# One pass over eight batches instead of two passes over four

## The chip, the cores and the metric

The kernel runs on one core of a Trainium2 chip. The time is the device time of one execution in microseconds (us), and the median of several runs is quoted. Five engines run their own streams of instructions and meet through semaphores: TensorE (PE, with its weight loads PEld), VectorE (DVE), ScalarE (ACT), GpSimd (POOL) and SyncE (SP), which issues the transfers here.

## The reference

x has 8 batches of 512 rows of 128 channels. Three layers are added onto it, each on the layer-normalised x:

```python
x = x + 0.5 * ffn(layernorm(x))       # FFN 1
x = x + latent_attention(layernorm(x))  # MLA
x = x + 0.5 * ffn(layernorm(x))       # FFN 2, same weights as FFN 1
```

Each ffn has two layers. One layer shifts half of the channels by one row, projects to q, k, v (8 heads of 64), normalises q and k, rotates them, attends in windows of 64 rows (this one and the one before), projects back and adds, then normalises and runs a gated feed-forward part of 341 hidden channels. The latent attention has 16 heads of 8 channels, a latent of 64, and full causal attention over the 512 rows. Nothing is exchanged between batches.

## The kernel before

**Staging.** Weights are loaded and prepared once, in a setup block. Then comes a hardware loop, line 1223, with B // NB = 2 rounds. X, the running activations, and U, the normalised copy and the ffn's own running value, hold NB = 4 batches in SBUF, NS = NB * NT = 16 slots of 128 rows. One round loads four batches (line 328), runs `ffn_phase`, `mla_phase` and `ffn_phase` on them, and stores them (line 335). Each phase is a block of its own with a barrier between all engines behind it, and `clear_all` (line 109) ends the round with semaphore clears and one more barrier. The loop body is written once in the program and run twice.

**The ffn phase.** A unit is one slot in one of the two layers; there are NU = 2 * NS = 32 units in a phase, all slots of layer 0 and then all of layer 1. `STEPS = range(NU + 7)`: a software pipeline written out by hand. In step n every engine does a piece of unit n, of n-1, and so on down to n-7, in an order fixed in the code. So the first steps fill the pipeline and the last seven drain it. On DVE a unit passes, among others, RA and RB (rotation, lines 647 and 651), SS (sum of squares over q and k, line 719, in step u+2), KT (740), the row maxima NMX (630), ON (756), GLU (685), and the new value of its slot, U (727, step u+7); in layer 1 the update of X follows (731). POOL does the sums RA, the powers RN and RV and the scalings. Two edits depend on the slot count: `norm_stats` of slot u+NT runs in steps with u+NT < NS, and `norm_apply` in steps NT <= u < NS, both on DVE. A slot of layer 1 waits for the U of the same slot in layer 0, which is NS units back.

**The MLA phase.** Per batch there are GROUPS = 4 groups of four heads, and per group UN = 11 score tiles. The phase runs ALLU = NB * 4 * 11 tiles and YT_LAG + 1 = 12 steps more. In the first group of a batch DVE also makes the norm of the next batch; XT, values, queries and keys of the next one are prepared between tiles. Before the first tile the first batch's norm, transpose, values, queries and keys run one after the other.

Ring buffers (RA, PT, KT and V for two batches, PSUM banks) do not depend on NB.

Of the kernel before, what the change touches and what calls it, by code (L numbers as in the profile page):

```python
# [16 lines left out]
P = 128  # L17
# [5 lines left out]
LG = 4  # L23
# [26 lines left out]
def macaron(nc, x, W_dq, W_uq, W_dkv, W_uk, W_uv, W_o, wqkv, q_scale, k_scale, wo, ln_g, ln_b,  # L50
            w1, b1, w2, b2, consts, out):
    B, T, C = x.shape
    DEPTH, HID = w2.shape[0], w2.shape[1]
    NT = T // P
    NB = 4
    NS = NB * NT
    QL = W_dq.shape[0]
    HC = -(-HID // 3)
# [4 lines left out]
    with top:  # L63
# [3 lines left out]
        def sb(name, shape, dt=F32):  # L67
            return stack[-1].enter_context(nc.sbuf_tensor(f"{name}_{phase[0]}", shape, dt))
# [3 lines left out]
        def sem(name, kind="setup"):  # L72

            if (kind, name) not in sems:
                sems[kind, name] = top.enter_context(nc.semaphore(f"{name}_{kind}"))
            return sems[kind, name]
# [2 lines left out]


        ROPE = NT * 4 * DH
        cst = sb("cst", [P, ROPE + 4 * P + LG + 2])
        ident = cst[:, ROPE + 3 * P:ROPE + 4 * P]
        headsel = cst[:, ROPE + 4 * P:ROPE + 4 * P + LG]
        low_rows = cst[:, ROPE + 4 * P + LG:ROPE + 4 * P + LG + 2]
        maskb = sb("maskb", [P, 3, P], BF16)
        identb = sb("identb", [P, P], BF16)
        ropet = sb("ropet", [P, DEPTH, NT, 4, DH])
# [20 lines left out]
        def clear_all(used):  # L109

            engines = (nc.sync, nc.tensor, nc.scalar, nc.vector, nc.gpsimd)
            for n, s in enumerate(used):
                engines[n % len(engines)].sem_clear(s)
            nc.all_engine_barrier()


        with ExitStack() as scope:
            stack.append(scope)
            qs = sb("qs", [P, DEPTH, 2, DH])
            ks = sb("ks", [P, DEPTH, DH])  # L120
            dq = sb("dq", [QL, P]); uq = sb("uq", [P, QL]); dkv = sb("dkv", [QL, P])
# [9 lines left out]
            with nc.Block() as block:  # L131
                @block.sync
                def _(sp):
                    def load(dst, src):
                        sp.dma_start(dst, src).then_inc(loaded, 16)
                        LOADS[0] += 16
                    load(cst[:, :], consts)
                    load(dq[:, :], W_dq); load(uq[:, :], W_uq); load(dkv[:, :], W_dkv)
                    load(uk[:, :], W_uk); load(uv[:, :], W_uv); load(wom[:, :], W_o)
                    load(wqkv_raw[:, :, :], wqkv.rearrange("l p n -> p l n"))  # L140
                    load(w1_s[:, :, :], w1.rearrange("l p n -> p l n"))
                    for l in range(DEPTH):
                        load(wo_s[:, l, :, :], wo[l].rearrange("(c p) n -> p c n", p=P))
                    for c in range(3):
                        load(w2_s[0:HCS[c], :, c, :], w2[:, c * HC:c * HC + HCS[c], :].rearrange("l p n -> p l n"))
                    load(b1row[:, :], b1.rearrange("l (e h) -> (l e) h", e=2))
                    load(lnrow[0:DEPTH, :], ln_g)
                    load(lnrow[DEPTH:2 * DEPTH, :], ln_b)
                    load(b2_s[:, :, :].rearrange("p l n -> p (l n)"),
                         b2.rearrange("(a l) n -> a (l n)", a=1).broadcast_to([P, DEPTH * P]))  # L150
                    load(qs[:, :, 0, :], q_scale.unsqueeze(0).broadcast_to([P, DEPTH, DH]))
                    load(qs[:, :, 1, :], k_scale.unsqueeze(0).broadcast_to([P, DEPTH, DH]))
# [47 lines left out]
                @block.vector  # L200
                def _(dve):

                    dve.wait_ge(loaded, NL)
                    nc.vector.tensor_copy(maskb[:, :, :], cst[:, ROPE:ROPE + 3 * P].rearrange("p (a b) -> p a b", a=3))
                    nc.vector.tensor_copy(identb[:, :], ident)
                    dve.wait_ge(mm, 3)
                    nc.vector.tensor_copy(lncol[:, :], BK[7][:, 0:2 * DEPTH]).then_inc(columns, 1)
                    for c in range(3):
                        last = nc.vector.tensor_copy(b1raw[0:HCS[c], c, :], BK[7][0:HCS[c], 8 * (c + 1):8 * (c + 1) + 2 * DEPTH])
                    last.then_inc(columns, 1)  # L210

                    def stacked(bank):
                        return bank[:, 0:P].rearrange("p (g e) -> p g e", g=GROUPS).unsqueeze(2) \
                            .to_broadcast([P, GROUPS, 4, LG * DG])

                    for n, (dst, src, factor) in enumerate([
                            (uqT[:, :], BK[0][0:QL, 0:P], 1.0), (woT[:, :], BK[1][:, 0:P], 1.0),
                            (WqT[:, :], BK[3][:, 0:P], 1.0),
                            (Wq_s[:, :, :, :], stacked(BK[4]), float(DG) ** -0.5),
                            (ve[:, :], BK[5][0:QL, 0:P], 1.0), (keT[:, :], BK[6][0:QL, 0:P], 1.0),  # L220
                            (Wv_s[:, :], BK[0][:, 0:P], 1.0), (Wk_s[:, :, :, :], stacked(BK[1]), 1.0)]):
                        dve.wait_ge(mm, [1, 2, 4, 5, 6, 7, 8, 9][n])
                        nc.vector.tensor_scalar(dst, src, factor, None, ALU.mult).then_inc(copied, 1)
                    for l in range(DEPTH):

                        tab = cst[:, 0:ROPE].rearrange("p (t f d) -> p t f d", t=NT, f=4)
                        for f in range(4):
                            sc = qs[:, l, f // 2, :]
                            if f % 2:
                                for hf in range(2):  # L230
                                    other = sc[:, (1 - hf) * 32:(1 - hf) * 32 + 32]
                                    nc.vector.tensor_tensor(
                                        ropet[:, l, :, f, hf * 32:hf * 32 + 32], tab[:, :, f, hf * 32:hf * 32 + 32],
                                        other.unsqueeze(1).to_broadcast([P, NT, 32]), ALU.mult)
                            else:
                                nc.vector.tensor_tensor(ropet[:, l, :, f, :], tab[:, :, f, :],
                                                        sc.unsqueeze(1).to_broadcast([P, NT, DH]), ALU.mult)
                    dve.wait_ge(mm, 10)
                    dve.wait_ge(columns, 2)
                    for l in range(DEPTH):  # L240
                        for c in range(3):
                            j = l * 6 + c
                            nc.vector.tensor_tensor(b1_s[0:HCS[c], l, :, c], BK[2][0:HCS[c], j:j + 4:3],
                                                    b1raw[0:HCS[c], c, 2 * l:2 * l + 2], ALU.add)

                        nc.vector.tensor_scalar(w1_s[:, l, :], w1_s[:, l, :], lncol[:, l:l + 1], None, ALU.mult)
# [24 lines left out]

        def ffn_phase(it, load, store, used):
            with ExitStack() as scope:
                stack.append(scope)

# [28 lines left out]
                    "w1a_in w1g_in gl_ok glu_ok w2_in u3_ok dch st nvar_ok nrstd_ok u_ok x_ok stored").split()}  # L306
                x_in = [sem(f"x_in{b}", "ffn") for b in range(NB)]
                NU = DEPTH * NS
# [14 lines left out]
                with nc.Block() as block:  # L323
                    @block.sync
                    def _(sp):
                        if load:
                            for b in range(NB):
                                sp.dma_start(X[:, b * NT:(b + 1) * NT, :],
                                             x[it * NB + b].rearrange("(t p) c -> p t c", p=P)).then_inc(x_in[b], 16)
                        for last_use in used:  # L330
                            sp.sem_clear(last_use)
                        if store:
                            for b in range(NB):
                                sp.wait_ge(S["x_ok"], NT * (b + 1))
                                sp.dma_start(out[it * NB + b].rearrange("(t p) c -> p t c", p=P),
                                             X[:, b * NT:(b + 1) * NT, :]).then_inc(S["stored"], 16)
                            sp.wait_ge(S["stored"], 16 * NB)

# [881 lines left out]
                phase[0] += 1  # L1220
                return list(S.values())

        with nc.Fori(0, B // NB, 1) as it:
            used = ffn_phase(it, load=True, store=False, used=[])
            used = mla_phase(used)
            clear_all(ffn_phase(it, load=False, store=True, used=used))


# [26 lines left out]
```

## Time and profile before

| | us |
|---|---|
| median of 3 runs | 2463.88 (2462.53 to 2465.33) |
| span of the profiled execution | 2459.3 |
| median less span | 4.6 |

| engine | busy us | share of the span |
|---|---|---|
| DVE | 2183.2 | 89% |
| PE | 2129.6 | 87% |
| ACT | 1663.2 | 68% |
| POOL | 1246.0 | 51% |

The page gives the span of the profiled execution, from the first to the last instruction, and no other time of it; the 4.6 us to the median lie around it. Busy is time in which an engine works on an instruction. The program has six phases that stand apart in the trace: ffn, MLA, ffn, and the same again, so a share of the whole span mixes three kinds of work with their beginnings and ends; the windows by phase are to be read instead.

### The profile page before, as it was taken

The numbers are of one execution on the slowest core, as the hardware profiler recorded it, in microseconds if no ns is written. First come the engines' busy times: TensorE is split into PE (matmuls) and PEld (weight loads), VectorE is DVE, ScalarE is ACT, GpSimd is POOL, SyncE is SP. The second block draws the span as 40 slices with busy tenths as digits, with TensorE's granted clock in tenths as the row PEclk, the third lists the DMA queues.
The fourth block names the chain that finished last, engine by engine and source line by source line (L and its number), as shares of the span: only waits on it lengthen the run. The fifth ranks groups of instructions, "written<-read, shape, count | busy, mean of one in ns | idle before, by whom it ended". The sixth has DMA issues, their size and how long they took to land. (4 is left out here: it accounts for less than half of the span.)

```text
span 2459.3 us, 58228 instructions
## 1 busy us (share of the span) xinstructions
PE 2129.6 (87%) x20074; PEld 1666.7 (68%) x20074; DVE 2183.2 (89%) x5134; ACT 1663.2 (68%) x3674; POOL 1246.0 (51%) x1048
## 2 busy tenths in 40 slices
PE   2888899879997988989968988998799978898997
PEld 2677777756664777777747777777466657777776
DVE  4999999968887999999969999998688879999997
ACT  1676767648895666776726677676588846777675
POOL 3656655523224565655545565564232256565553
PEclk9999999979998999999979999999899989999999
DMA  2000000000000000000000000000000000000000
GB/s 89 1 2 2 2 2 1 2 1 1 2 1 1 1 2 2 1 2 10 6 23 2 2 1 2 2 2 1 1 2 1 1 1 1 2 2 2 6 6 10
DMA packets 12619, 12.41 MB, mean 5 GB/s; under 512 B 1397, under 2 KB 11687, under 8 KB 12327
## 3 DMA queue, kind: packets, MB, share of 16 engines
q1 hardware_dynamic: 12327, 8.63, 1.2%
q8 instruction: 170, 2.79, 0.5%
q14 instruction: 122, 1.00, 0.1%
HBM read 6.53 MB, written 2.10 MB: 4 GB/s over the span
## 5 line engine op out<-in xcount | busy, mean ns | idle before, releaser
L847 POOL TENSOR_TENSOR RN<-SS,mhalf 128x16 f32<-128x16 f32 x128 | 374.9, 2929 | 19.1 <-DVE SS L721 19.0
L838 POOL TENSOR_TENSOR U2B<-U,b_s 128x128 f32<-128x128 f32 x128 | 61.3, 479 | 569.7 <-DVE U L727 555.4
L539 ACT ACTIVATE PR<-bank,NMX 128x128 f32<-128x128 f32 x1024 | 290.1, 372 | 56.3 <-DVE NMX L632 51.9
L596 ACT ACTIVATE GL<-bank,b_s 114x128 f32<-114x128 f32 (+1 forms) x384 | 113.3, 366 | 251.7 <-PE bank L386 251.7
L377 PE MATMUL bank<-KT,QZ 128*64 128x128 f32 x4096 | 280.5, 279 | 0.0
L377 PEld LDWEIGHTS bank<-KT,QZ 128*64 128x64 f32 x4096 | 218.7, 137 | 70.0 <-issue 70.0
L1092 ACT ACTIVATE PL<-bank,NM 128x384 f32<-128x384 f32 (+3 forms) x512 | 255.9, 542 | 14.0 <-DVE NM L1170 11.2
L1170 DVE TENSOR_REDUCE NM<-bank 128x1 f32<-128x384 f32 (+3 forms) x352 | 217.3, 635 | 38.6 <-PE bank L1006 34.9
L386 PE MATMUL bank<-HN,w_s 128*114 128x128 f32 (+1 forms) x1536 | 222.9, 282 | 0.0
L362 PE MATMUL bank<-wqkv_h,HTH 128*128 128x512 f32 x384 | 196.9, 513 | 11.1 <-DVE HTL L707 11.0
L1015 PE MATMUL bank<-cst,PL 128*128 128x128 f32 x1280 | 200.1, 275 | 3.9 <-ACT PTL L1084 1.9
L386 PEld LDWEIGHTS bank<-HN,w_s 128*114 128x114 f32 (+1 forms) x1536 | 186.2, 180 | 19.9 <-issue 19.9
L1001 PE MATMUL bank<-KL,QZL 128*128 128x384 f32 (+3 forms) x512 | 190.5, 425 | 4.6 <-DVE QZL L1129 4.6
L578 ACT ACTIVATE PT<-bank 128x512 f32<-128x512 f32 x128 | 76.5, 597 | 160.8 <-PE bank L444 160.4
L630 DVE TENSOR_REDUCE NMX<-bank 128x4 f32<-128x512 f32 x256 | 174.8, 683 | 10.8 <-PE bank L377 9.5
L647 DVE TENSOR_TENSOR RA<-bank,ropet 128x512 f32<-128x512 f32 x256 | 174.5, 681 | 9.0 <-PE bank L362 4.8
L353 PE MATMUL bank<-cst,RA 128*128 128x128 f32 x1024 | 163.6, 285 | 12.2 <-POOL RA L858 11.3
L651 DVE TENSOR_TENSOR RB<-bank,ropet 128x512 f32<-128x512 f32 x256 | 173.6, 678 | 0.0
L1210 POOL TENSOR_SCALAR QZL<-QS,cst 128x512 fp32r<-128x512 f32 x64 | 108.1, 1699 | 128.7 <-DVE QS L1119 128.5
L1084 ACT ACTIVATE PTL<-bank 128x512 f32<-128x512 f32 (+1 forms) x288 | 162.1, 563 | 13.9 <-PE bank L1015 10.4
L476 PEld LDWEIGHTS bank<-VA,PT 128*64 128x64 f32 x2048 | 135.6, 143 | 48.7 <-issue 48.7
L830 POOL TENSOR_TENSOR RA<-RA,RB 128x512 f32<-128x512 f32 x128 | 162.1, 1267 | 10.8 <-DVE RB L651 10.8
(159 smaller groups left out, 6238.9 us busy)
## 6 DMA issues: line engine op xcount, KB each, us to landing
X<-in_L_attn_x SPq DMA_DIRECT2D x8, 256.0 KB, 4.3
out<-X SPq DMA_DIRECT2D x8, 256.0 KB, 2.3
wqkv_raw<-in_L_ffn_wqkv SPq DMA_DIRECT2D x1, 1536.0 KB
cst<-shape_constants SPq DMA_DIRECT2D x1, 771.0 KB
w_s<-in_L_ffn_w SPq DMA_DIRECT2D x1, 682.0 KB
wo_s<-in_L_ffn_wo SPq DMA_DIRECT2D x2, 256.0 KB
w_s<-in_L_ffn_w SPq DMA_DIRECT2D x2, 114.0 KB
b_s<-in_L_ffn_b SPq DMA_DIRECT2D x1, 128.0 KB
```

What stands on the lines that cost most here:

```text
L362: last = nc.tensor.matmul(BK[B_QKV[k]][:, :], h[:, bb, tok].bitcast(F32R), w[:, l, cols].bitcast(F32R), start=(n == 0), stop=(n == 2))
L377: last = nc.tensor.matmul(BK[B_S[g]][w * W:(w + 1) * W, (h % 4) * P:(h % 4 + 1) * P], QZ[:, h, w * W:(w + 1) * W], KT[:, h // 2, bb, k0:k0 ...
L386: last = nc.tensor.matmul(BK[k][0:HCS[j], j * P:(j + 1) * P], w1_s[:, l, o:o + HCS[j]], HN[:, :], start=True, stop=True)
L539: last = nc.scalar.activation(PR[:, 4 * g + h, :], BK[B_S[g]][:, h * P:(h + 1) * P], ACT.Exp, bias=NMX[:, 4 * g + h:4 * g + h + 1], scale=8.0)
L630: link(nc.vector.tensor_reduce(c, BK[B_S[g]][:, :].rearrange("p (h q) -> p h q", h=4), AX_X, ALU.max))
L647: nc.vector.tensor_tensor(RA[:, u % 2, g, :, :], src, ropet[:, l, t, 2 * g, :].unsqueeze(1).to_broadcast([P, NH, DH]), ALU.mult)
L651: nc.vector.tensor_tensor(RB[:, g, :, :].rearrange("p h (z d) -> p h z d", z=2), rot, tab.unsqueeze(1).to_broadcast([P, NH, 2, DH // 2]), ...
L847: nc.gpsimd.tensor_tensor(RN[:, u % 2, :], SS[:, :], mhalf[:, 0:2 * NH], ALU.pow).then_inc(S["rn_ok"], 1)
L1001: nc.tensor.matmul(bank[:, h * N:(h + 1) * N], QZL[:, G % 2, h0 + h, i * P:(i + 1) * P].bitcast(F32R), KL[:, G % 2, 0:N].bitcast(F32R), st ...
L1015: last = pe.transpose(BK[B_PT[k % 2]][:, j * P:(j + 1) * P], PL[:, k % PRING, j * P:(j + 1) * P], ident)
L1092: last = nc.scalar.activation(PL[:, m % PRING, h * N:(h + 1) * N], BK[m % SRING][:, h * N:(h + 1) * N], ACT.Exp, bias=NM[:, m % SRING, h:h ...
L1170: nc.vector.tensor_reduce(NM[:, m % SRING, 0:n], BK[m % SRING][:, 0:n * N].rearrange("p (h k) -> p h k", h=n), AX_X, ALU.max, negate=True) ...
```

## The change

NB becomes B = 8: the hardware loop and its `it` index are gone, and each phase is written out for 32 slots, 64 ffn units and 352 tiles of latent attention. The loads and stores address x[b] and out[b] directly. X and U are twice as large in SBUF; to make room the rotation table is loaded into a tile `rope` of its own, which lives only during setup, with one more load.

```diff
-    NB = 4
+    NB = B
...
-        cst = sb("cst", [P, ROPE + 4 * P + LG + 2])
-        ident = cst[:, ROPE + 3 * P:ROPE + 4 * P]
+        cst = sb("cst", [P, 4 * P + LG + 2])
+        ident = cst[:, 3 * P:4 * P]
...
+            rope = sb("rope", [P, ROPE])
...
-                    load(cst[:, :], consts)
+                    load(rope[:, :], consts[:, 0:ROPE])
+                    load(cst[:, :], consts[:, ROPE:])
...
-                        tab = cst[:, 0:ROPE].rearrange("p (t f d) -> p t f d", t=NT, f=4)
+                        tab = rope[:, :].rearrange("p (t f d) -> p t f d", t=NT, f=4)
...
-        def ffn_phase(it, load, store, used):
+        def ffn_phase(load, store, used):
...
-                                             x[it * NB + b].rearrange("(t p) c -> p t c", p=P)).then_inc(x_in[b], 16)
+                                             x[b].rearrange("(t p) c -> p t c", p=P)).then_inc(x_in[b], 16)
...
-                                sp.dma_start(out[it * NB + b].rearrange("(t p) c -> p t c", p=P),
+                                sp.dma_start(out[b].rearrange("(t p) c -> p t c", p=P),
...
-        with nc.Fori(0, B // NB, 1) as it:
-            used = ffn_phase(it, load=True, store=False, used=[])
-            used = mla_phase(used)
-            clear_all(ffn_phase(it, load=False, store=True, used=used))
+        used = ffn_phase(load=True, store=False, used=[])
+        used = mla_phase(used)
+        clear_all(ffn_phase(load=False, store=True, used=used))
```

Where it moves instructions is shown at three places. First the end of the last ffn phase on SP, with the waits of each row: before, each round ends with four stores, clears, and the branch back to the loads.

```order
L331 ISA x29
L335 ISA [waits x_ok_ffn]
L335 DMA out<-X 128x4x128
...
L323 UNCONDITIONAL_BRANCH [waits stored_ffn]
L113 ISA [waits barrier_Pool_Activation_PE_DVE_SP_release]
L113 ISA x13
L1223 REGISTER_ALU [waits barrier_Pool_Activation_PE_DVE_SP_release]
L1223 COMPARE_AND_BRANCH
```

The same place now, where the eight stores of the single pass follow each other and nothing branches back:

```order
L333 ISA x29
L337 DMA out<-X 128x4x128 [waits x_ok_ffn] x8
L325 UNCONDITIONAL_BRANCH [waits stored_ffn]
L113 ISA [waits barrier_Pool_Activation_PE_DVE_SP_release]
L113 ISA x14
```

One store wait, one barrier and the branch in the middle of the run are gone. Second, DVE at the last update of X of batch 3 in the second ffn phase (slot 15); X is written at L731 before and at L733 after. Before, the pipeline has drained and DVE has the last units' GLU, U and X alone:

```order
L701 TENSOR_TENSOR HN<-bank,DT 128x128
L727 TENSOR_TENSOR U<-bank,U2B 128x128
L731 SCALAR_TENSOR_TENSOR X<-U,X 128x128
L685 SCALAR_TENSOR_TENSOR GLU<-bank,b_s,GL 114x128 x2
L685 SCALAR_TENSOR_TENSOR GLU<-bank,b_s,GL 113x128
L727 TENSOR_TENSOR U<-bank,U2B 128x128
L731 SCALAR_TENSOR_TENSOR X<-U,X 128x128
L323 UNCONDITIONAL_BRANCH
```

Now the work of later slots stands around the same update:

```order
L709 TENSOR_TENSOR HTL<-bank,HTH 64x128 x2
L662 COPY HT_3<-bank 64x128
L663 COPY HT_3<-bank 64x128
L721 TENSOR_REDUCE SS<-SQ 128x16
L723 TENSOR_SCALAR SS<-SS 128x16
L729 TENSOR_TENSOR U<-bank,U2B 128x128
L733 SCALAR_TENSOR_TENSOR X<-U,X 128x128
L742 COPY KT<-bank 128x4x128
L757 RECIPROCAL RS<-bank 128x4
L758 TENSOR_TENSOR ON<-bank,RS 128x256
```

Seven draining steps, and the filling ones behind them, have become full steps. Third, DVE in the MLA phase at the end of batch 3 (OTL is the copy of a group's result, Y its division, NM a row maximum). Before:

```order
L1170 TENSOR_REDUCE NM<-bank 128x1 x3
L1190 RECIPROCAL RL<-bank 128x16
L1193 TENSOR_TENSOR Y<-bank,RL 128x128
L1179 COPY PTL<-bank 128x4x128 x2
L1185 COPY OTL<-bank 128x512
L1190 RECIPROCAL RL<-bank 128x16
L1193 TENSOR_TENSOR Y<-bank,RL 128x128
L934 UNCONDITIONAL_BRANCH
```

Now:

```order
L1172 TENSOR_REDUCE NM<-bank 128x1
L1187 COPY OTL<-bank 128x512
L271 TENSOR_SCALAR U<-X,mv,rstd 128x128
L1172 TENSOR_REDUCE NM<-bank 128x1
L271 TENSOR_SCALAR U<-X,mv,rstd 128x128
L1172 TENSOR_REDUCE NM<-bank 128x1
L271 TENSOR_SCALAR U<-X,mv,rstd 128x128
L1172 TENSOR_REDUCE NM<-bank 128x1
L1192 RECIPROCAL RL<-bank 128x16
L1195 TENSOR_TENSOR Y<-bank,RL 128x128
```

The copy of batch 3's last result now stands among tiles and norm steps of the batches behind it.

## Rows read from the trace of the kernel before

**Rows 1.** The page: busy time by engine, and the clock in slices.

```profile
PE 2129.6 (87%) x20074; PEld 1666.7 (68%) x20074; DVE 2183.2 (89%) x5134; ACT 1663.2 (68%) x3674; POOL 1246.0 (51%) x1048
PEclk9999999979998999999979999999899989999999
```

**Rows 2.** Windows: us, busy (count) of PE, PEld, DVE, ACT, POOL; granted clock, DMA share, GB/s.

```profile
42.10:517.90 475.80, 413.64 (x4128) 341.08 (x4128) 445.18 (x1088) 313.79 (x699) 275.22 (x233) 0.98 0.01 3
517.90:767.80 249.90, 232.68 (x1760) 147.54 (x1760) 195.37 (x377) 200.68 (x437) 68.02 (x54) 0.95 0.01 1
767.80:1244.60 476.80, 414.85 (x4128) 342.08 (x4128) 445.13 (x1087) 313.70 (x699) 275.84 (x233) 0.96 0.01 3
1244.60:1254.20 9.60, 0.00 (x0) 0.00 (x0) 0.00 (x0) 1.23 (x1) 0.00 (x0) 0.55 0.28 72
1254.20:1730.20 476.00, 414.64 (x4128) 341.11 (x4128) 446.45 (x1088) 313.95 (x700) 275.44 (x233) 0.97 0.01 3
1730.20:1980.00 249.80, 232.60 (x1760) 147.29 (x1760) 194.84 (x376) 200.66 (x437) 68.33 (x54) 0.95 0.01 1
1980.00:2453.90 473.90, 411.81 (x4128) 339.57 (x4128) 444.67 (x1087) 313.89 (x699) 275.92 (x233) 0.97 0.01 3
```

**Rows 3.** Windows: one ffn batch, its drain, one MLA batch, its start.

```profile
96.20:153.90 57.70, 51.76 (x518) 42.40 (x517) 55.39 (x139) 40.72 (x90) 32.75 (x27) 0.98 0.01 2
478.20:517.90 39.70, 34.66 (x346) 29.50 (x344) 27.58 (x86) 20.08 (x45) 10.38 (x12) 0.92 0.01 1
618.20:675.20 57.00, 56.45 (x441) 35.87 (x441) 47.92 (x94) 50.04 (x110) 16.64 (x13) 1.00 0.01 2
518.40:542.30 23.90, 12.68 (x34) 7.26 (x35) 11.20 (x29) 5.70 (x12) 7.24 (x6) 0.50 0.00 1
```

**Rows 4.** Tile SS on DVE, five starts a window: ns min/median/max, first and last start.

```profile
L719 DVE TENSOR_REDUCE SS<-SQ x5: 1219/1219/1220, 96.2 to 153.9; 128x16 f32<-128x1024 f32 x5
L719 DVE TENSOR_REDUCE SS<-SQ x5: 1219/1220/1222, 267.1 to 322.3; 128x16 f32<-128x1024 f32 x5
L719 DVE TENSOR_REDUCE SS<-SQ x5: 1219/1219/1222, 379.3 to 436.4; 128x16 f32<-128x1024 f32 x5
L719 DVE TENSOR_REDUCE SS<-SQ x5: 1219/1220/1221, 1049.8 to 1106.2; 128x16 f32<-128x1024 f32 x5
```

**Rows 5.** Tile OTL on DVE, five starts, one for each group.

```profile
L1185 DVE COPY OTL<-bank x5: 691/692/692, 618.2 to 675.2; 128x512 f32<-128x512 f32 x5
```

**Rows 6.** Timeline between the rounds: start, us, engine, line.

```profile
1244.74 0.37 SPq L335 DMA_DIRECT2D out<-X  x1
1250.09 3.94 SPq L328 DMA_DIRECT2D X<-in_L_attn_x  x4
1254.25 0.29 DVE L254 BATCH_NORM_STATS2 stats<-X 128x6 f32<-128x128 f32 x1 [9.68 <-DMA X<-in_L_attn_x]
```

**Rows 7.** Timeline of the setup and of the first round's start.

```profile
1.21 0.56 SPq L135 DMA_DIRECT2D dq<-in_L_attn_W_dq  x1
...
24.44 0.36 DVE L204 CAST maskb<-cst 128x384 bf16<-128x384 f32 x1 [24.44 <-DMA qs<-in_L_ffn_k_scale]
...
39.23 2.10 SPq L328 DMA_DIRECT2D X<-in_L_attn_x  x4
42.10 0.29 DVE L254 BATCH_NORM_STATS2 stats<-X 128x6 f32<-128x128 f32 x1 [3.88 <-DMA X<-in_L_attn_x]
```

**Rows 8.** The page: DMA queues that carry instructions.

```profile
q8 instruction: 170, 2.79, 0.5%
q14 instruction: 122, 1.00, 0.1%
```

**Rows 9.** Line L968 on PE in two windows, 518.4 to 542.3 and 618.2 to 675.2.

```profile
L968 PE MATMUL bank<-XT,Wq_s x4: 1061/1062/1220, 529.0 to 540.5; 128*128 128x512 f32 x4
...
L968 PE MATMUL bank<-XT,Wq_s x8: 592/594/595, 624.2 to 667.1; 128*128 128x512 f32 x8
```

**Rows 10.** Timeline: the last entry of the run.

```profile
2454.19 0.37 SPq L335 DMA_DIRECT2D out<-X  x1
```

More of the change, by code:

```diff
@@ L81, in macaron @@
         ROPE = NT * 4 * DH
-        cst = sb("cst", [P, ROPE + 4 * P + LG + 2])
-        ident = cst[:, ROPE + 3 * P:ROPE + 4 * P]
-        headsel = cst[:, ROPE + 4 * P:ROPE + 4 * P + LG]
-        low_rows = cst[:, ROPE + 4 * P + LG:ROPE + 4 * P + LG + 2]
+        cst = sb("cst", [P, 4 * P + LG + 2])
+        ident = cst[:, 3 * P:4 * P]
+        headsel = cst[:, 4 * P:4 * P + LG]
+        low_rows = cst[:, 4 * P + LG:4 * P + LG + 2]
         maskb = sb("maskb", [P, 3, P], BF16)
@@ L203, in _ @@
                     dve.wait_ge(loaded, NL)
-                    nc.vector.tensor_copy(maskb[:, :, :], cst[:, ROPE:ROPE + 3 * P].rearrange("p (a b) -> p a b", a=3))
+                    nc.vector.tensor_copy(maskb[:, :, :], cst[:, 0:3 * P].rearrange("p (a b) -> p a b", a=3))
                     nc.vector.tensor_copy(identb[:, :], ident)
```

## The prediction

> **What bounds the kernel now.** I read the page first, then the windows by phase, then the distance between the same instruction in successive batches. The page has DVE at 2183.2 us of 2459.3 and PE at 2129.6 [rows 1]. That looks like a kernel with nothing left to gain, and it is misleading: it averages stretches in which one engine is full with stretches in which none is. The windows show six phases and a gap: 475.8, 249.9, 476.8, then 9.6 us in which no engine but ACT shows work, then 476.0, 249.8, 473.9 [rows 2].
>
> Inside a phase there is a steady part. In an ffn batch of 57.7 us DVE is busy 55.39, so DVE sets the pace there; in an MLA batch of 57.0 us PE is busy 56.45, so PE does [rows 3]. At the ends of a phase neither holds: in the last 39.7 us of the first ffn phase DVE is busy 27.58, and in the first 23.9 us of MLA PE is busy 12.68 and DVE 11.20, at a granted clock of 0.50, the lower of TensorE's two levels (1.2 of 2.4 GHz) [rows 3]. What the pipelines lose there is paid per phase, whatever the number of batches in it. The change halves the number of phases and doubles their length, so all turns on the difference between a phase and its batches at steady pace.
>
> **What a batch costs at steady pace.** SS is reduced once in a unit, in step u+2, so five starts in a row span four units, which is one batch in one layer [rows 4]:
>
> - layer 0, units 4 to 8, steps 6 to 10: 153.9 - 96.2 = 57.7 us. All four steps hold both norm edits (statistics run while n < 12, the apply while 4 <= n < 16).
> - layer 1, units 16 to 20: 322.3 - 267.1 = 55.2. No norm and hardly any update of X.
> - layer 1, units 24 to 28: 436.4 - 379.3 = 57.1, with the update of X in each; and in the third phase units 20 to 24, 1106.2 - 1049.8 = 56.4, three of four units with it.
>
> With 32 slots the norm statistics run while n < 28 and the apply while n < 32, so the 16 units added to layer 0 all carry both norm edits, and the 16 added to layer 1 all carry the update of X. I take 57.7 and 57.1. An ffn phase thus becomes longer by 4 x 57.7 + 4 x 57.1 = 459.2 us. In MLA the copy OTL comes once in a group, four groups are a batch: 675.2 - 618.2 = 57.0, with the norm of the next batch in it [rows 5]. The last batch alone has no such norm, before and after. MLA becomes longer by 4 x 57.0 = 228.0 us.
>
> **The change part by part.**
>
> 1. First ffn phases. Before, 475.8 + 476.0 = 951.8 [rows 2]. After, one fill and drain plus everything steady: 475.9 (mean of the two) + 459.2 = 935.1. Saved 16.7.
> 2. MLA. Before 249.9 + 249.8 = 499.7 [rows 2]; after 249.85 + 228.0 = 477.85. Saved 21.85. More than in ffn, since MLA's start is a chain through all engines at the lower clock [rows 3], while the ffn fill has short steps.
> 3. Last ffn phases. Before 476.8 + 473.9 = 950.7 [rows 2]; after 475.35 + 459.2 = 934.55. Saved 16.15.
> 4. The gap between the rounds: wait for the last store, clears, barrier, branch back, load of the next four batches, and DVE's wait for the first of them. The store is issued at 1244.74, the load at 1250.09, and DVE starts at 1254.25 [rows 6]. All of the 9.6 us [rows 2] go. The stores of batches 0 to 3 are issued in mid-phase and lie beside compute: SP has nothing queued behind them but the next store. The last store of the run stays where it was, from 2454.19 to the end of the span, 5.1 us [rows 10].
> 5. Setup: one more load on SP. The issues stand 0.5 to 0.6 us apart (dq's takes 0.56), and DVE and PE start only when the last load, k_scale, has landed at 24.44 [rows 7]. Cost between 0 (if the bytes, which stay the same, set that landing) and 0.6 (if the issues do); I take 0.5, since k_scale is issued last.
> 6. X loads: eight in a row instead of four. DVE waits for batch 0 alone, which landed 2.9 us after the issue in the first round (39.23 to 42.10) and 4.2 us in the second (1250.09 to 1254.25) [rows 6, 7]. Batch 1 is wanted in the first step, each later one four steps, some 57 us, after the one before it, so the rest is covered. If the eight shared the queues so evenly that batch 0 landed with twice the second figure, that would cost up to 5.5 us; I take 0, as the DVE start 2.9 us after the first issue, with four loads queued over 2.10 us, shows no such sharing. It could also land up to 1 us earlier, as static addresses need no register work ahead of each issue; no row separates that, and it stays in the range.
> 7. Larger X and U, the table in a tile of its own, higher semaphore counts, four more clears on SP in MLA: no instruction on DVE or PE is added by them. At 0; a clear on SP delays nothing that DVE or PE wait for inside the phase.
>
> Sum: 16.7 + 21.85 + 16.15 + 9.6 - 0.5 = **63.8 us**. The span goes from 2459.3 to 2395.5. With the same 4.6 us to the median around it, the time is **2400**, a ratio of 0.974 to the 2463.88.
>
> **What the doubled program costs.** The loop body is written once and runs twice; now it is straight code of twice the length. The instruction queues brought 2.79 + 1.00 = 3.79 MB [rows 8] for the 58228 instructions executed, 65 bytes each, so the loop did not save the second fetch: both rounds were already streamed from memory, and the same bytes flow now. The second round's first ffn phase took 476.0 us against 475.8 [rows 2], so neither being first nor being second costs anything. The Trainium skill ("Runtime: NRT & Kernel Launch", section "Instruction fetch mechanics") says that code need not fit an engine's instruction memory, as it is streamed in blocks of 256 instructions of 64 bytes, and that a taken branch breaks the prefetch; the 65 bytes agree with it, and by it a part of the 9.6 us gap is such a stall, which the sum already holds.
>
> **The rivals.**
>
> *Steady pace improves too (2390).* The spread of rows 4 shows batches without their small stalls: 56.4 instead of 57.1 in layer 1. If, away from phase ends, the eight added batches of layer 1 took 56.4 and the eight of layer 0 57.1, that (as much less again) gives 8 x 0.7 + 8 x 0.6 = 10.4 us more, 2390. For it: the granted clock is 0.98 in a steady batch, not 1.00 [rows 3]. Against it: the two rounds repeat each other within 0.2 us in MLA and the first ffn phase, so the stalls belong to the order of the code.
>
> *Steady pace gets worse (2419).* The stretches added are ones that no run has had: units 32 and up. If each of the 64 added ffn units lost 0.3 us, half of the (57.7 - 55.2) / 4 = 0.6 us by which units of rows 4 differ, by a POOL or a PE that falls behind little by little, the time is 2400 + 19 = 2419. For it: PE is busy 51.76 and DVE 55.39 of 57.7, a narrow margin. Against it: buffers and their waits are the same rings, and the batch from 379.3 is no slower than that from 96.2 [rows 4], hundreds of us into a phase.
>
> *Nothing moves (2455 to 2464).* The drained steps would only be free if the next phase's start were hidden behind them. It can't be: every phase ends in a barrier, and the windows show it. What speaks for a small rest is that only the gap must vanish in any case: 2464 - 9.6 + 0.5 = 2455.
>
> *Slower: the clock of TensorE (over 2500).* Before, PE never works for longer than 477 us without a slack stretch at a phase's end. If the clock fell to its lower level because of the length of the work, it would stay there. The same matmul took 1062 ns at a granted clock of 0.50 and 594 ns in full-clock MLA [rows 9], a factor of 1.79. PE's 51.76 us of an ffn batch would be 92.6, which then sets the pace instead of 57.7: 35 us more a batch. It decides from 63.8 / 35 = 1.8 batches at the low level; four of them give 2400 + 140 = 2540, slower than before. Against it: the row for MLA's steady batch has the clock at 1.00 with PE busy 56.45 of 57.0, and the low stretch of rows 3 comes behind a drain with PE idle in part; the clock falls where PE pauses, not where it works. The Trainium skill ("TensorE: Matmul & The Clock Gate", section "What's actually happening") describes the low level as the default from which activity releases the array; by that rule this rival gets no chance, and the rows agree.
>
> **How the numbers follow.** The forecast, 2400 with 2394 to 2407 as its own range (each of the eight steady terms is read to 0.1 us, the fill of an ffn phase differs by up to 2.9 us between 476.8 and 473.9, the load may cost up to 5.5): 0.74. Better steady pace, around 2390: 0.09. Worse steady pace, around 2419: 0.11. Nothing or nearly nothing moves: 0.03. Slower through the clock: 0.03. The range of 2390 to 2416 leaves out both extremes and the outer halves of the two pace rivals, some 0.14. A change of 0.2%, 5 us, is about what a measurement of this kernel can tell from none. Faster by more than that: 0.74 + 0.09 + 0.11 and half of the fourth case, 0.955; within it 0.015; slower 0.03.
>
> **What would show each step.** In the profile after: three phases with no gap between 42 and about 2390; the first ffn phase 935 us long, MLA 478, the last ffn phase 935; SS starts 57.7 apart for five starts in layer 0 up to the sixth batch and 57.1 in layer 1; OTL starts 57.0 apart through seven batches; stretches at a clock of 0.5 behind setup and at two phase changes, not at five; the first DVE work behind setup at 24.9 and X's at 42.6. The prediction is wrong if the distance of SS or OTL starts grows in the second half of a phase, if the window of MLA is over 481 us, or if the start of X's first statistics moves by more than 1 us.

## The result, and the profile after

| | before | after |
|---|---|---|
| median us (first comparison, 4 runs each) | 2464.54 | 2396.82 |
| lowest to highest | 2462.53 to 2465.33 | 2395.76 to 2398.42 |
| span of the profiled execution | 2459.3 | 2396.6 |

The ratio is 0.9731, with a 95% interval of 0.9718 to 0.9745: faster by 67.7 us. Forecast were 2400 us and a saving of 63.8 us.

The page of after: span and count of instructions, busy time by engine, and the clock in its 40 slices.

```profile
span 2396.6 us, 58054 instructions
...
PE 2115.1 (88%) x20074; PEld 1660.4 (69%) x20074; DVE 2178.8 (91%) x5128; ACT 1672.6 (70%) x3681; POOL 1235.7 (52%) x1036
...
PEclk9999999999999999899999998999999999999999
```

Against [rows 1] the busy times are nearly the same (DVE 2178.8 us for 2183.2, PE 2115.1 for 2129.6, both for the same 20074 matmuls): no work went away, only time in which none was done. PE's 14.5 us less go with a mean granted clock of 0.975 over the span, where before had 0.965. The slices of the clock show two dips, at the two phase changes, where [rows 1] had one at each of five.

Windows of after by phase, with the columns of [rows 2]:

```profile
42.10:975.40 933.30, 820.58 (x8256) 677.84 (x8256) 889.24 (x2172) 633.99 (x1403) 547.28 (x461) 0.98 0.01 3
975.40:1453.40 478.00, 458.64 (x3520) 291.14 (x3520) 388.96 (x752) 400.75 (x873) 133.17 (x106) 0.98 0.01 1
1453.40:2391.20 937.80, 826.51 (x8256) 683.36 (x8256) 888.63 (x2170) 633.84 (x1403) 547.98 (x461) 0.97 0.01 4
```

Three phases in place of six and no gap. 933.3, 478.0 and 937.8 us stand against forecasts of 935.1, 477.85 and 934.55. The first is 1.8 us short and the last 3.3 us long.

The pace inside, as in [rows 4] and [rows 5]: SS in two batches of layer 0 that only the longer phase has with both norm edits, SS in layer 1 from unit 55 to unit 59 of 64, and OTL in MLA's fifth batch.

```profile
L721 DVE TENSOR_REDUCE SS<-SQ x5: 1219/1220/1220, 211.6 to 269.5; 128x16 f32<-128x1024 f32 x5
L721 DVE TENSOR_REDUCE SS<-SQ x5: 1219/1220/1221, 269.5 to 327.7; 128x16 f32<-128x1024 f32 x5
L721 DVE TENSOR_REDUCE SS<-SQ x5: 1220/1220/1221, 824.6 to 881.3; 128x16 f32<-128x1024 f32 x5
```

```profile
L1187 DVE COPY OTL<-bank x5: 691/692/692, 1246.8 to 1303.8; 128x512 f32<-128x512 f32 x5
```

These are 57.9, 58.2, 56.7 and 57.0 us, where 57.7, 57.7, 57.1 and 57.0 had been read from before. The pace did not drift, 800 us into a phase. The second ffn phase has one batch of layer 1 that stands out, 57.8 us behind one of 56.7. DVE is busy as long in both; PE is not, and the granted clock is 0.95 in the slower one and 0.99 in the other:

```profile
2138.80:2195.50 56.70, 49.72 (x516) 41.72 (x515) 54.96 (x132) 39.94 (x89) 33.56 (x28) 0.99 0.02 6
2195.50:2253.30 57.80, 52.64 (x519) 43.98 (x518) 54.89 (x132) 39.68 (x89) 33.58 (x28) 0.95 0.02 6
```

### The profile page after: what moved, and what is told of

Same layout as the page of the kernel before. It is cut to its first block and busy times, and to the rows that moved or that the text cites. A ratio compares the mean times of both kernels' runs of the same rounds, so it can differ in the third digit from the quotient of the medians.

```text
span 2396.6 us, 58054 instructions
## 1 busy us (share of the span) xinstructions
PE 2115.1 (88%) x20074; PEld 1660.4 (69%) x20074; DVE 2178.8 (91%) x5128; ACT 1672.6 (70%) x3681; POOL 1235.7 (52%) x1036
## 3 DMA queue, kind: packets, MB, share of 16 engines
q8 instruction: 169, 2.77, 0.5%
## 5 line engine op out<-in xcount | busy, mean ns | idle before, releaser
L541 ACT ACTIVATE PR<-bank,NMX 128x128 f32<-128x128 f32 x1024 | 290.1, 372 | 49.2 <-DVE NMX L634 45.6
```

The costliest lines, as they stand in the source:

```text
L541: last = nc.scalar.activation(PR[:, 4 * g + h, :], BK[B_S[g]][:, h * P:(h + 1) * P], ACT.Exp, bias=NMX[:, 4 * g + h:4 * g + h + 1], scale=8.0)
```

## The experiments

All times below are medians; before took 2464.11, 2463.94 and 2462.88 us in the three comparisons that they come from (1 to 4, 5 to 8, and 9 to 11 with the second run of 8).

**1. The loop written out.** Same six phases, same store and load between the rounds.

```diff
-        with nc.Fori(0, B // NB, 1) as it:
+        for it in range(B // NB):
```

> The kernel before with its hardware loop written out as two rounds in straight code; batches per phase, barriers, store and load between the rounds stay. If the gain comes from the number of phases and not from the loop, as I hold, this gives at most what the branch back and the register work ahead of each load cost: the gap between the rounds goes from 9.6 us to 7 to 9, the phases keep 476, 250 and 475 us, and the time is 2461 to 2464 us. Rival, the loop itself costs (a refetch of code after the branch, or time outside the span that only a looping program has, since the medians moved by 67.7 us and the spans by 62.7): then this is 4 us or more faster, 2460 or less, and its time stands no more than 2 us above its span.

Measured: 2457.48 us (10 runs), ratio 0.9974 (0.9965 to 0.9984) to before, 6.6 us faster. The gap in its timeline:

```profile
1246.45 0.37 SPq L335 DMA_DIRECT2D out<-X  x1
1251.17 2.74 SPq L328 DMA_DIRECT2D X<-in_L_attn_x  x4
1254.68 0.29 DVE L254 BATCH_NORM_STATS2 stats<-X 128x6 f32<-128x128 f32 x1 [8.25 <-DMA X<-in_L_attn_x]
```

DVE waits 8.25 us here and 9.68 in [rows 6], and the span from the last store's issue to the load's issue is 4.7 us, not 5.35. So the gap accounts for 1.4 of the 6.6 us. More was gained than I expected of the loop's removal, and the rival's number came true. Its second mark, a time no more than 2 us above the span, tells nothing: each execution here stands 1.9 to 2.0 us above its span, and so does each of before. The other 5 us do not lie in the gap. They are a difference of medians, not a fixed price of the loop: in the last comparison three of nine executions of before took 2456.6 to 2459.0 us, within the 2454.7 to 2461.3 of the ten runs here, at a mean granted clock of 0.967 to 0.970. Experiments 5 and 11 come back to them.

**2. No transfers between the rounds.** X holds eight batches; all loads stand at the start, the stores of the first round are not waited for.

```diff
+                            for b in range(NB):
+                                sp.dma_start(X_all[:, (NB + b) * NT:(NB + b + 1) * NT, :],
+                                             x[NB + b].rearrange("(t p) c -> p t c", p=P)).then_inc(late_in[b], 16)
...
-                            sp.wait_ge(S["stored"], 16 * NB)
+                            if b0:
+                                sp.wait_ge(late_out, 32 * NB)
```

> Still two rounds of four batches in straight code, six phases, but X holds all eight batches, all loads are issued at the start and the stores of the first round are not waited for. It removes the gap's store and load and nothing else. The theory: the gap shrinks from 9.6 us to what clears and a barrier take, 1 to 3 us, and the time is 2464.5 - 7 to 8.5 = 2456 to 2458 us, so that the gap is a seventh of the gain. Rival, the transfers between the rounds are the main cost, through the idle they leave and the lower TensorE clock in the phase behind them: then the first ffn phase of the second round shortens too, and the time is 2445 us or less.

Measured: 2453.56 us, ratio 0.9957 (0.994 to 0.9974). The gap now, on its timeline:

```profile
1241.41 0.29 DVE L747 SCALAR_TENSOR_TENSOR X<-U,X 128x128 f32<-128x128 f32 x1
1241.73 0.37 SPq L350 DMA_DIRECT2D out<-X  x1
1244.43 0.29 DVE L258 BATCH_NORM_STATS2 stats<-X 128x6 f32<-128x128 f32 x1 [2.73 <-PEq L116]
```

DVE waits 2.73 us, for the clears and the barrier alone. The gap is 6.9 us shorter than in before, of which 1.4 had gone with the loop. The time is 3.9 us under that of experiment 1, where the gap is 5.5 us shorter (four runs here, 3.4 us apart, don't settle the difference), and 2.4 under my expected range, which had not counted what the loop costs outside the gap. The rival, 2445 us or less, is out: loop and transfers together are 10.5 us, a sixth of the gain, and six short phases still cost 2453.6 - 2396.8 = 56.8 us more than three long ones, the medians being of two chips. So the gain of 67.7 us in the medians is made up of some 6.6 for the loop, 3.9 for the transfers and 56.8 for the phases, with 2.7 us of clears and a barrier in the last.

**3. MLA alone in two passes.** On the kernel after:

```diff
-        used = mla_phase(0, NB, used)
+        clear_all(mla_phase(0, NB // 2, used))
+        used = mla_phase(NB // 2, NB // 2, [])
```

> The kernel after with the latent attention alone in two passes of four batches, with clears and a barrier between them; both ffn phases keep eight batches. The theory: the term for MLA, 21.85 us, comes back, plus 1 to 2 us for the clears: two MLA windows of 250 us each in place of one of 478, and 2396.8 + 23 = 2420 us (2418 to 2422). Rival, the terms are not additive (a phase gains from its neighbours' length): under 2412 us.

Measured: 2420.79 us, +24.0, inside the expected 2418 to 2422. Its windows:

```profile
978.20:1229.20 251.00, 232.73 (x1760) 147.46 (x1760) 194.89 (x376) 200.41 (x437) 68.32 (x54) 0.95 0.01 1
1229.20:1478.70 249.50, 231.97 (x1760) 147.16 (x1760) 194.74 (x377) 198.97 (x436) 68.79 (x54) 0.96 0.01 1
```

251.0 + 249.5 - 478.0 = 22.5 us for the term forecast at 21.85, with clears and a barrier of some 2 us in it. In the two passes PE is busy 464.7 us and idle 35.8, in the one pass of after 458.6 and 19.4: 16.4 us are idle time paid once more, and 6.1 us are the same matmuls run slower, behind a second start at the lower clock (0.95 and 0.96 for 0.98 over the window).

**4. The first ffn phase alone in two passes.**

```diff
-        used = ffn_phase(0, NB, load=True, store=False, used=[])
+        clear_all(ffn_phase(0, NB // 2, load=True, store=False, used=[]))
+        used = ffn_phase(NB // 2, NB // 2, load=True, store=False, used=[])
```

> The kernel after with the first ffn phase alone in two passes of four batches, with clears and a barrier between them; the loads of batches 4 to 7 stand in the second pass. The theory: the two passes take 476 us each against the one of 933.3, which is 18.7 us (16.7 by the forecast), plus 3 to 6 us for clears, barrier and the wait for a load behind them: 2396.8 + 23 = 2420 us (2416 to 2424). Rival, fill and drain of the ffn phase cost little and most of the saving in that phase is the load wait: under 2410 us.

Measured: 2420.39 us, +23.6, inside 2416 to 2424.

```profile
42.80:517.80 475.00, 413.09 (x4128) 339.33 (x4128) 446.12 (x1087) 313.81 (x699) 275.17 (x233) 0.99 0.01 3
517.80:523.10 5.30, 0.00 (x0) 0.00 (x0) 0.00 (x0) 0.00 (x0) 0.00 (x0) 0.55 0.33 99
523.10:998.90 475.80, 413.48 (x4128) 340.15 (x4128) 444.93 (x1087) 315.11 (x700) 275.20 (x233) 0.97 0.01 3
```

475.0 + 475.8 - 933.3 = 17.5 us are fill and drain (forecast 16.7), and 5.3 us the wait for clears, barrier and load, the row with no busy engine. The rival, under 2410 us, is out.

**5. The kernel before, profiled again.** No edit.

> The kernel before once more, for a second profiled execution. Every execution so far took 1.8 to 2.0 us more than its span, so that the execution profiled first, with a span of 2459.3, was one of 2461.2 and not of the median 2464.1. One theory: what differs between executions is the granted clock of TensorE at the ends of phases, since longer executions have a lower mean clock; then the phases differ by 1 to 2 us each, the batches inside them by less than 0.5 us. Rival: the gap between the rounds varies (code and data fetched from memory), by 2 us or more. If this execution is again under 2461 in span, neither is told apart.

Measured: a span of 2465.3 us, 6.0 more than in the first profile. The first four units of a phase, from the first start of SS to the fifth, take 45.5 us here. The window in this execution:

```profile
54.60:100.10 45.50, 38.38 (x295) 29.06 (x296) 40.89 (x86) 21.72 (x56) 33.14 (x25) 0.87 0.00 1
```

The same stretch in the first profile:

```profile
53.30:96.20 42.90, 33.99 (x295) 25.45 (x296) 40.67 (x87) 21.89 (x56) 33.02 (x25) 0.95 0.01 1
```

The counts on PE are the same, DVE's busy time too (40.89 and 40.67 us), but PE is busy 38.38 us and not 33.99, at a granted clock of 0.87 and not 0.95. A steady batch takes about what it took before: here units 4 to 8, with SS from 100.1 to 157.9, 57.8 us against the 57.7 of [rows 4]; over all batches of both profiles the same one differs by 0.6 us at most.

The two gaps differ by 0.1 us, so the second theory is out. Over the four fills the second execution is 3.7 us longer and its first DVE work on X comes 1.3 us later. The first theory holds in part: from the first statistics to the next phase's, or to the last X, three of the six phases differ by 1.1 to 2.3 us and three by 0.6 or less. A fill is not all of a phase: the first one is 2.6 us longer here, but the drain behind it, from the last SS to the last update of X, is 37.7 us at a clock of 0.96 where the first profile has 38.8 at 0.92. Over all profiles whose ffn drain has no added instructions it takes 36.3 to 37.2 us at a granted clock of 1.00, 37.6 to 38.3 at 0.96 and 38.8 to 39.2 at 0.92 or 0.93. The mean clocks of the two profiled executions, 0.965 and 0.964, hardly differ, so it matters where the low level falls. The 28 executions of before in the first two comparisons show the same in bulk: time and mean granted clock have a correlation of -0.84. That is a correlation and a comparison of profiles, not an edit; experiment 8 makes the edit for one seam.

**6. The change in the other direction.** Before, with `NB = 2`: four rounds of two batches.

> The kernel before with NB = 2: four rounds of two batches, the change made in the other direction. If a round's fixed part (fill, drain, start of MLA, gap) is 64 to 67 us whatever its length, this costs two more of them: 2464 + 2 x 66 = 2596 us (2588 to 2604). Rival: with 8 slots a unit of layer 1 needs the value of a unit only 8 steps back, which is written 7 steps behind its own start, so the pipeline has one step of slack and could stall at the seam: over 2606 us. Second rival: the fixed parts shrink, as their norms and memory clears are smaller: under 2585 us.

Measured: 2595.36 us, ratio 1.0536 (1.0519 to 1.0552). Two rounds more cost 131.4 us, 65.7 each, in the middle of the expected 64 to 67; both rivals are out, the one step of slack at the seam of the layers included. With 67.7 us for one round less, a round costs nearly the same (within 3%) whether it holds two, four or eight batches; both figures hold what the loop costs.

**7. The next norm in the drain.** On the kernel after: statistics, power and apply of the next phase's first batch are moved ahead of the barrier. In the ffn phase (MLA likewise):

```diff
+                            if load and n in (NU + 1, NU + 2):
+                                dve.wait_ge(S["x_ok"], NT)
+                                for t in (0, 1) if n == NU + 1 else (2, 3):
+                                    norm_stats(dve, S, t, NS + t)
+                            if load and n in (NU + 4, NU + 5):
+                                for t in (0, 1) if n == NU + 4 else (2, 3):
+                                    norm_apply(dve, S, t, NB)
```

> The kernel after, and the norm of the next phase's first batch is made in the drain of the phase before it, where DVE has idle time. In the profile after, the first transpose of MLA stands some 6.4 us behind its phase's first norm instruction, that of the last ffn phase 3.7 us. The theory: fixed parts are chains that nothing hides, so what is taken out of the chain is gained: -5.5 and -3.3 us, 2396.8 - 9 = 2388 us (2386 to 2390). Rival: in the drain DVE is itself in the chain (GLU, U, X), so the moved instructions, about 3.2 us of them at each place, are paid there: 2393 us or more.

Measured: 2392.36 us, 4.3 under the kernel after of experiment 9 (another chip), between the theory's 2388 and the rival's 2393, and nearer to the rival. The profiles show both at work. At the first seam, from the last update of X to the first row maximum of MLA it is 978.8 to 993.2 = 14.4 us, where after has 974.8 to 996.0 = 21.2; but from the last SS to that update it is 938.6 to 978.8 = 40.2 us where after has 36.9. So 6.8 us are gained behind the seam and 3.3 are given back ahead of it. Not all of the 3.3 need be DVE's added work on the chain: the drain ran at a clock of 0.96 here and 1.00 in after, and drains without the added norm took 37.6 us or more at 0.96. The second seam pays too: from MLA's last Y to the first SS it is 1450.3 to 1457.6 = 7.3 us for 12.3 in after, and MLA up to that Y is 0.9 longer, a net gain of 4.2. The profiled execution, 2388.96 us, was the fastest of the five, so its 3.5 + 4.2 us are more than the median shows.

**8. Matmuls on constants at the start of MLA.** On the kernel after, so that PE's clock does not fall:

```diff
+                        def keep_warm(k):
+                            for _ in range(k):
+                                nc.tensor.matmul(BK[B_O][:, 0:3 * P], identb[:, :], maskb[:, :, :].rearrange("p a b -> p (a b)"),
+                                                 start=True, stop=True, skip_group_check=True)
+                        keep_warm(18)
                         xt(0)
+                        keep_warm(3)
                         values(0)
+                        keep_warm(3)
                         queries(0)
+                        keep_warm(7)
                         keys(0)
+                        keep_warm(7)
```

> The kernel after, and while PE waits at the start of MLA it runs matmuls on constants into a bank that is overwritten later (38 of 384 columns), so that the granted clock is not at its lower level for the 23.9 us there. The theory that the low clock is a part of MLA's fixed cost: PE's chain of 1.1 + 2.05 + 2.07 + 2.08 us before the first tile goes at up to twice the pace, and the first tiles too: -3 to -6 us, 2391 to 2394 us. Rival: the clock costs nothing there, since the chain is one of waits on ACT and DVE, or the added matmuls stand in the way: 2396 us or more.

Measured: 2396.45 us, which alone would be the rival's number. The first real matmuls on PE in its timeline, with what each waited for:

```profile
983.70 0.66 PE L956 MATMUL bank<-cst,U 128*128 128x128 f32 x4 [1.64 <-DVE U L271]
...
985.23 1.13 PE L963 MATMUL bank<-Wv_s,XT 128*128 128x128 f32 x8 [0.39 <-DVE XT L1123]
...
987.05 1.12 PE L970 MATMUL bank<-XT,Wq_s 128*128 128x512 f32 x2 [0.20 <-ACT VL L1060]
...
989.64 1.12 PE L976 MATMUL bank<-XT,Wk_s 128*128 128x512 f32 x2 [0.33 <-DVE QS L1130]
```

And the same in after:

```profile
981.80 1.11 PE L956 MATMUL bank<-cst,U 128*128 128x128 f32 x4 [7.39 <-DVE U L271]
983.79 2.04 PE L963 MATMUL bank<-Wv_s,XT 128*128 128x128 f32 x8 [0.88 <-DVE XT L1114]
986.52 2.07 PE L970 MATMUL bank<-XT,Wq_s 128*128 128x512 f32 x2 [0.69 <-ACT VL L1051]
990.07 2.08 PE L976 MATMUL bank<-XT,Wk_s 128*128 128x512 f32 x2 [1.47 <-DVE QS L1121]
```

The same work takes 4.03 us instead of 7.30. The granted clock is 0.93 in the 24 us from 977.0, where after has 0.50 in the 23.9 us from 975.8. From the last update of X to the first row maximum it is 976.7 to 994.3 = 17.6 us, not 21.2. The edit was therefore run again next to the kernel after:

> The matmuls on constants at the start of MLA alone, once more, beside the kernel after on the same chip. In the first profile the start of MLA, from the end of the phase before to the first row maximum, took 17.6 us instead of 21.2, but the median, 2396.45, was that of the kernel after on another chip. Theory that the clock is worth its 3.6 us: 3 to 4 us faster than the kernel after beside it. Rival: it is given back elsewhere: within 1 us of it.

Measured: 2393.25 us beside 2396.64, 3.4 us faster. Over both comparisons, 10 runs with the added matmuls have a mean of 2394.8 us and 9 of the kernel after 2396.8: 2.0 us, give or take 1.4 (95%). The low clock at this seam is a cost, then, of 3.6 us in the stretch itself in both profiles and of 2.0 in the mean; whether the rest is given back elsewhere is not shown.

**9. The kernel after again.** No edit, as the measure of this comparison.

> The kernel after once more, on the same chip as the three next to it, as their measure. 2396 to 2398 us. Its profile shows how far the fills of its two ffn phases vary: the theory that what varies between executions is the clock at phase ends says that the batches in layer 0 and 1 stay at 57.7 and 57.2 us within 0.3 and the fills take 43 to 46 us up to the fifth SS.

Measured: 2396.64 us; the fills are 43.7 and 45.5 us, the batches of layer 0 with both norm edits 57.6 to 58.1, those of layer 1 56.6 to 57.3. The mark on the fills holds; that on the batches is missed by up to 0.3 us by a few. The last ffn phase is 934.3 us from its first statistics to its last update of X, against 938.0 in the first profile of this kernel. The fills are the same, 45.5 and 45.4 us. The drain is not, here and then in the first profile:

```profile
2352.00:2389.20 37.20, 31.88 (x343) 27.04 (x341) 27.55 (x85) 20.05 (x45) 10.27 (x12) 1.00 0.03 9
2352.40:2391.70 39.30, 34.92 (x347) 29.85 (x345) 27.51 (x85) 20.05 (x45) 10.40 (x12) 0.93 0.03 8
```

DVE's busy time is equal, and the drain is 2.1 us longer where the granted clock is 0.93. The batches account for the rest.

**10. Both remedies.** The norm in the drain, with its statistics and applies now ahead of the last four updates of U, and the matmuls of experiment 8 with 4 ahead of `xt(0)`.

```diff
+                            if load and n in (NU + 3, NU + 4):
+                                dve.wait_ge(S["x_ok"], NT)
+                                for t in (0, 1) if n == NU + 3 else (2, 3):
+                                    norm_stats(dve, S, t, NS + t)
+                            if load and n in (NU + 5, NU + 6):
+                                for t in (0, 1) if n == NU + 5 else (2, 3):
+                                    norm_apply(dve, S, t, NB)
                             u = n - 7
```

> Both remedies for the fixed parts in one kernel: the next phase's first norm in the drain before it, now placed where DVE waits for PE (ahead of the last four updates of U) and not at the ends of full steps, and matmuls on constants while PE waits at the start of MLA. The first placement gained 6.8 us behind the first seam and gave 3.3 back in the drain ahead of it. Theory: that return is a matter of placement, so 2 to 3 us of it stay, and the clock adds 2 to 3 more: 2396.8 - 4.5 - 2.5 - 2 = 2387 to 2389 us. Rival: DVE's drain has no room anywhere and the clock is worth nothing in the median: 2392 us, as with the norm alone.

Measured: 2386.06 us (5 runs, 2382.49 to 2388.89), 10.6 us under the kernel after on the same chip, ratio to before 0.9687 (0.9674 to 0.97): the fastest version of this study. Its reason is only half of mine. From the last SS to the last X it takes 939.9 to 979.8 = 39.9 us, 3.0 more than in after and hardly less than the 40.2 of experiment 7. That need not be the placement: the clock was 0.92 in this drain, at which drains without the added norm took 38.8 to 39.2 us, so the two can't be told apart. The statistics of slots 2 and 3 take 1.1 us in a step in which after waits 0.39. Behind the seam 8.2 us are gained, 979.8 to 992.8 = 13.0 for 21.2, and at the second seam a net 3.6 (8.2 for 12.3, less 0.5 in MLA). In the medians the two edits together bring 10.6 us, more than their sum of 4.3 and 2.0 to 3.4; in the profiles the seams bring 8.8, less than the 11.3 of experiments 7 and 8. This is not settled; the ranges of the runs, 6 us wide, leave room for chance.

**11. The kernel after in a loop of one round.**

```diff
+        with nc.Fori(0, B // NB, 1) as it:
+            used = ffn_phase(it, load=True, store=False, used=[])
...
```

> The kernel after inside a hardware loop of a single round, with the loads and stores addressed through the loop's index. Writing out the loop of the kernel before gained 6.6 us in the median where the gap showed 1.4. If the cost lies in the second round (the branch back, its refetch, what follows it), a loop that never branches back costs 0 to 1.5 us here: 2397 to 2398.5 us. Rival: the form of the code costs (register work ahead of each load, entry of the loop, the start of the first phase): 2400 us or more.

Measured: 2398.38 us, 1.7 us above the kernel after beside it, with runs that overlap (2395.43 to 2399.77 and 2395.14 to 2397.94). The rival's 2400 is missed, the theory's 1.5 nearly met: a loop's form costs at most a little, and most of the 6.6 us of experiment 1 seems to need a second round.

## Why the prediction was right, point by point

- **What bounds the kernel.** Right. The page looked full at 89%, and 2.7% were to be had, since the loss sat at phase ends. Experiment 6 shows it from the other side: a round more costs 65.7 us.
- **Steady pace.** Right: 57.7, 57.1 and 57.0 us had been read, and the added batches took 57.6 to 58.2, 56.7 to 57.8 and 57.0. Both rivals on the pace fell as forecasts of the time. But the reason given for the faster one has something in it: with the update of X a batch takes 56.7 us at a granted clock of 0.99 and 57.8 at 0.95 with DVE equally busy, so the pace is not DVE's alone, and the small stalls do not all belong to the order of the code.
- **First ffn phases, 16.7.** From the windows 951.8 - 933.3 = 18.5; experiment 4, with one edit, 17.5. **MLA, 21.85**: 499.7 - 478.0 = 21.7; experiment 3, 22.5. **Last ffn phases, 16.15**: 950.7 - 937.8 = 12.9. This is the term furthest off, and most of the miss belongs to the profiled execution: experiment 9 has this phase 3.7 us shorter, which makes the term 16.6, with a drain of 36.9 us for 39.1. Its fill, 1464.6 to 1510.0 = 45.4 us up to the fifth SS, is no accident of one execution: it is 45.2 to 45.6 in all eight profiles with MLA in one pass, and 43.8 to 45.5 in the two of before, so about 1 us of the term may be lost for good.
- **The gap, 9.6.** Gone, as the windows show. That it was all store, load and barrier was not right: the loop had 1.4 us of it (experiment 1), the transfers 5.5 (the rest of experiment 2), clears and barrier 2.7.
- **Setup, 0.5.** No cost shows, but none of 0.5 us could. The last load did land later, at 24.8 us and not 24.4, and DVE's first work on X starts at 42.1 in both profiles; over all profiles that start lies anywhere between 42.0 and 43.4. The eight loads cost nothing: DVE starts 2.9 us after their first issue, as before.
- **The doubled program.** It costs nothing, as [rows 8] had it: q8 and q14 bring 2.77 and 0.95 MB after, for 2.79 and 1.00. The direction was missed: the straight code is the faster form by 6.6 us in experiment 1, when two rounds are kept. The sum had only the 1.4 us of it that lie in the gap.
- **The slower rival.** Out. The granted clock is 0.98 in 933 us of one phase. The clock did matter, in the other sense: fewer starts at its lower level.
- **From the span to the time.** This step failed, with a small error. I added the 4.6 us between span and median to both. Every execution since shows 1.6 to 2.3 us around its span, and those of before 1.9 to 2.0. The profiled execution of before was therefore, by estimate, one of about 2461.2 us (2459.3 + 1.9), 3 us faster than the median, with a short first fill (42.9 us, up to where [rows 4] begin). The spans differ by 62.7 us where 63.8 was forecast; the medians by 67.7. The median of after came out 3.2 us below the forecast mostly for this reason: 4.6 less 1.8 is 2.8. That the rest is so small is in part luck: in the profile the first ffn phase was 1.8 us under its forecast and the last 3.3 over.

What stays open: where the 5 us of experiment 1 outside the gap lie. The ffn phases of its second round were shorter than those of experiment 5's profile by 4.6 and 2.3 us, in fills and drains for the most part, and shorter than those of the first profile of before by 2.2 and 0. Its mean clock is higher (0.967 against 0.964, the means over 10 and 13 executions). Whether the branch back causes this, or the time at which the second round starts, was not separated.

## What to carry to other kernels

A loop over phases pays the fill, drain and first chain of each phase in every round; compare a phase's window with its number of batches times the steady distance between equal instructions, and the difference, with the gap between the rounds here 64 us a round by forecast, is what a longer phase saves. What a round costs stayed the same within 3% from two batches to eight, so the first doubling of the phase length brings most. A single profile's span must be set against its own execution's time, and an execution's place among the others matters when terms of 2 or 3 us are summed. Before a change of 2 or 3 us in a fill or drain is put down to an edit, compare the granted clock of the two stretches.

## What the hardware showed that I had not expected

- The fill of one and the same ffn phase took 42.9 us at a mean granted clock of 0.95 and 45.5 us at 0.87, while DVE, which sets the steady pace, had equal busy time; the same steady batch differed by 0.6 us at most. The drain of that phase goes with the clock in the same way, 36.9 us at 1.00 and 39.1 at 0.93. The steady pace is not free of it either, though DVE seems to set it: 56.7 us a batch at 0.99, 57.8 at 0.95.
- 38 matmuls on constants kept the granted clock up through MLA's start and cut its real matmuls from 7.30 to 4.03 us, worth 2.0 us of the mean time, give or take 1.4.
- A hardware loop of two rounds cost 6.6 us more in the median than the same two rounds in straight code, 1.4 us of it at the seam itself; where the rest arises is not shown.
